# A hybrid attention and expert layer on one core: keys of two head groups packed in one tile, and the rounded products of an attention slot in one run ahead of its attended product

## What is computed

```
x = x + attn_a(layernorm(x))      16 heads, DK = 16, DV = 64
x = x + ffn(layernorm(x))         32 experts (top 8, grouped), one shared expert
x = x + attn_b(layernorm(x))      32 softmax taps of a banded sum
x = x + ffn(layernorm(x))

attn_a:  q, k, v = l2norm of the heads of x@Wq, x@Wkv
         sim  = q . k  per head            (256 x 256)
         attn = square(relu(sim))
         out  = tanh_norm(attn @ v)        tanh(|o|) * o/|o|
         return out (heads side by side) @ Wout
```

## Time and profile before

| | |
|---|---|
| median of 3 runs | 580.83 us (580.67 to 581.53) |
| profiled execution | 580.82 us, of which the span is 579.0 us |
| mean granted TensorE clock | 0.984 |
| busy in the span | PE 536.2 us (93%), PEld 407.0, DVE 424.5, ACT 381.3, POOL 329.6 |
| attention stage | to about 240 us; its batches b=2, 3 start their first factor product at 79.11 and 107.15 us |
| expert stage | from 241.5 us |

### The profile page before, as it was taken

How to read it: one execution, slowest core, us unless ns; L and a number is a source line. 1 busy time by engine, 2 the same in 40 slices (tenths; PEclk the granted TensorE clock), 3 DMA queues, 4 the chain that set the end, 5 groups by cost and what they waited for, 6 DMA issues and landing times. The chain is left out here.

```text
span 579.0 us, 10233 instructions
## 1 busy us (share of the span) xinstructions
PE 536.2 (93%) x3328; PEld 407.0 (70%) x3328; DVE 424.5 (73%) x998; ACT 381.3 (66%) x681; POOL 329.6 (57%) x279
## 2 busy tenths in 40 slices
PE   4678989999999998799999999999999999999996
PEld 4446556666666676487788787787787787888884
DVE  3827697877878688557958869669669668677664
ACT  4749868686868795454565775775775775655653
POOL 1527567483939293167646756656645656566563
PEclk9879999999999999889999999999999999999999
DMA  8200000000000000750076391580660761761930
GB/s 244 69 7 22 9 21 17 16 15 15 15 15 23 13 18 16 183 119 2 5 160 133 102 196 26 138 162 25 166 135 23 168 133 42 170 144 33 214 69 19
DMA packets 35797, 44.89 MB, mean 78 GB/s; under 512 B 5408, under 2 KB 18848, under 8 KB 35744
## 3 DMA queue, kind: packets, MB, share of 16 engines
q1 hardware_dynamic: 31328, 42.66, 32.4%
q10 hardware_dynamic: 4416, 1.57, 1.1%
HBM read 41.07 MB, written 3.15 MB: 76 GB/s over the span
## 5 line engine op out<-in xcount | busy, mean ns | idle before, releaser
L480 POOL TENSOR_TENSOR hl<-hb,hh 128x512 fp32r<-128x512 f32 x128 | 165.4, 1293 | 137.4 <-ACT hh L686 130.7
L679 ACT ACTIVATE sil<-PS 128x512 f32<-128x512 f32 (+1 forms) x136 | 80.8, 594 | 84.8 <-PE PS L1150 84.0
L1029 DVE TENSOR_TENSOR PS<-sil,PS 128x512 f32<-128x512 f32 x128 | 88.3, 690 | 60.3 <-PE PS L1150 38.9
L1150 PE MATMUL PS<-fxh,wfh 128*128 128x512 f32 x264 | 104.8, 397 | 1.7 <-issue 1.7
L1150 PE MATMUL PS<-fxh,wfl 128*128 128x512 f32 x264 | 104.5, 396 | 0.0
L1150 PE MATMUL PS<-fxl,wfh 128*128 128x512 f32 x264 | 104.5, 396 | 0.0
L686 ACT ACTIVATE hh<-hb 128x512 fp32r<-128x512 f32 x128 | 80.3, 628 | 33.1 <-DVE hb L1034 32.7
L1034 DVE TENSOR_TENSOR hb<-PS,wbc 128x512 f32<-128x512 f32 x128 | 88.5, 691 | 11.8 <-issue 3.6
L837 DVE SCALAR_TENSOR_TENSOR aT<-PS,rl 128x1024 f32<-128x1024 f32 x64 | 75.2, 1218 | 8.5 <-ACT rl L543 8.5
L543 ACT ACTIVATE rl<-PS 128x1024 f32<-128x1024 f32 x64 | 62.3, 1031 | 17.7 <-PE PS L1150 17.2
L1150 PE MATMUL PS<-aT,v 128*64 128x256 f32 x512 | 64.0, 393 | 6.0 <-POOL v L409 4.8
(11 more groups left out here) (163 smaller groups left out, 926.0 us busy)
## 6 DMA issues: line engine op xcount, KB each, us to landing
wbc<-w_dram SPq DMA_DIRECT2D x48, 512.0 KB, 11.7
wbc<-w_dram SPq DMA_DIRECT2D x32, 128.0 KB, 2.9
wbc<-w_dram SPq DMA_DIRECT2D x16, 256.0 KB, 4.4
wfs<-wf_dram SPq DMA_DIRECT2D x32, 98.0 KB, 1.9
band_dram<-zero SPq DMA_DIRECT2D x16, 80.0 KB, 1.7
band<-band_dram ACTq DMA_DIRECT2D x4, 320.0 KB, 3.0
out_dram<-X SPq DMA_DIRECT2D x4, 256.0 KB, 2.3
X<-x_dram SPq DMA_DIRECT2D x1, 896.0 KB, 8.1
```

The lines of the kernel that those rows point to most:

```text
L480: g.tensor_tensor(hl[:, n % RING, :], hb[:, n % RING, :], hh[:, n % RING, :].bitcast(F32), ALU.subtract).then_inc(F("hl"), 1)
L679: s.activation(sil[0:rows, n % 2, :], PS[0:rows, G0 + n % 2, :], ACT.Silu).then_inc(F("silu"), 1)
L1029: v_.tensor_tensor(PS[:, bank, :], sil[:, n % 2, :], PS[:, bank, :], ALU.mult).then_inc(F("t"), 1)
L1150: return nc.tensor.matmul(o, w, m, start=start, stop=stop)
```

## The change

Three things are done.

1. *Packed keys.* The 16 rows of zeros in a head's slot of 32 are used: the keys of groups 0 and 1 (and of 2 and 3) stand in the two halves of one key tile, and the queries of a group stand in its half with zeros in the other. So a batch has six tiles of 128 columns (Q0, Q1, K01, K23, Q2, Q3) in NQ = 3 group products for eight tiles in four. Weights have 256 columns less, ACT keeps three copies for four. `score` reads a key tile and a query tile and waits for both.
2. *Order.* The two `values(n, 0, *)` move ahead of `attend(4b)` on PE and ahead of `keep_output(4b)` on ACT; `values(n, 1, 1)` moves ahead of `transpose_norms`; the third group product moves ahead of `attend(4b+2)`, its copy ahead of `keep_output(4b+2)`. The list of turns follows. DVE's order stays as it is.
3. *Factor products.* `spread_factors` does two groups at a time, taking turns between them, and waits for both banks first.

The diff:

```diff
@@ -37,7 +37,10 @@
 BW = P + K
 QK = H * DK
 
-WQ_G, WK_G, W_QK, W_V = 0, NG * P, 2 * NG * P, 2 * NG * P + 2 * QK
+NQ = NG // 2 + 1
+WQ_G, WK_G = (0, 1, 4, 5), (2, 3)
+W_QK = 2 * NQ * P
+W_V = W_QK + 2 * QK
 WA = W_V + H * DV
 
 WG0, WU0, WD0, WS0 = 0, NE * P, 2 * NE * P, 3 * NE * P
@@ -84,15 +87,15 @@
     def late(q, *names):
         return list(names) if q >= 0 else []
 
-    order += [("g", 0, g) for g in range(NG)] + [("qk", 0, 0), ("qk", 0, 1)]
+    order += [("g", 0, j) for j in range(NQ)] + [("qk", 0, 0), ("qk", 0, 1)]
     order += [("v", 0, 0, 0), ("v", 0, 0, 1), ("v", 0, 1, 0), ("v", 0, 1, 1), ("xT", 1)]
     for b in range(B):
         n, q, r = b + 1, b - 1, b - 2
         order += late(r, ("F", r, 2), ("F", r, 3))
         order += coming(n, ("qk", n, 0), ("qk", n, 1), ("v", n, 0, 0), ("v", n, 0, 1)) + late(q, ("nb", q))
-        order += coming(n, ("v", n, 1, 0)) + late(q, ("nt", q)) + coming(n, ("v", n, 1, 1))
+        order += coming(n, ("v", n, 1, 0), ("v", n, 1, 1)) + late(q, ("nt", q))
         order += ([("px", 0)] if b == B - 2 else []) + ([("pc", 0)] if b == B - 1 else []) + late(r, ("y", r, 0))
-        order += coming(n, ("g", n, 0), ("g", n, 1), ("g", n, 2), ("g", n, 3))
+        order += coming(n, ("g", n, 0), ("g", n, 1), ("g", n, 2))
         order += coming(n + 1, ("xT", n + 1)) + late(q, ("ft", q)) + late(r, ("y", r, 1))
         order += ([("pl", 0)] if b == B - 2 else []) + late(q, ("F", q, 0), ("F", q, 1))
     for k, job in enumerate(order):
...
@@ -529,10 +532,10 @@
                 after(act, A("n2q"), 2 * (n - 1) + t + 1)
                 s.activation(sqqk[:, t, :], PS[:, bank_of("qk", n, t), :], ACT.Square).then_inc(free_of("qk", n, t), 1)
 
-            def keep_group(n, g):
-                act.wait_ge(*full("g", n, g))
-                after(act, A("S"), 2 * (NG * (n - 1) + g + 1))
-                s.activation(qk[:, g, :], PS[:, bank_of("g", n, g), :], ACT.Copy).then_inc(free_of("g", n, g), 1)
+            def keep_group(n, j):
+                act.wait_ge(*full("g", n, j))
+                after(act, A("S"), 2 * (NG * (n - 1) + (2 if j == 0 else NG)))
+                s.activation(qk[:, j, :], PS[:, bank_of("g", n, j), :], ACT.Copy).then_inc(free_of("g", n, j), 1)
 
             def relu(i):
                 if i >= NS:
...
@@ -622,10 +624,9 @@
                 if more:
                     square_pairs(n, 0)
                     square_pairs(n, 1)
-                keep_output(NG * b)
-                if more:
                     keep_values(n, 0, 0)
                     keep_values(n, 0, 1)
+                keep_output(NG * b)
                 if b:
                     keep_norms(q)
                 weight_high(NG * b)
@@ -648,10 +649,8 @@
                 if more:
                     keep_group(n, 0)
                     keep_group(n, 1)
+                    keep_group(n, 2)
                 keep_output(NG * b + 2)
-                if more:
-                    keep_group(n, 2)
-                    keep_group(n, 3)
                 if b:
                     tanh_norms(q)
                 weight_high(NG * b + 2)
@@ -1182,10 +1181,10 @@
                 bank, done = turn("qk", n, t)
                 by_token(n, t, W_QK, bank).then_inc(done, 1)
 
-            def group(n, g):
-                bank, done = turn("g", n, g)
-                for part, w0 in enumerate((WQ_G, WK_G)):
-                    cols = slice(w0 + g * P, w0 + (g + 1) * P)
+            def group(n, j):
+                bank, done = turn("g", n, j)
+                for part in range(2):
+                    cols = slice((2 * j + part) * P, (2 * j + part + 1) * P)
                     last = split3(PS[:, bank, part * L:(part + 1) * L], wah[:, cols], wal[:, cols],
                                   xTh[:, :], xTl[:, :])
                 last.then_inc(done, 1)
@@ -1194,13 +1193,15 @@
                 if i >= NS:
                     return
                 b, g = divmod(i, NG)
-                pe.wait_ge(*freed("g", b, g))
+                jq, q0, k0 = WQ_G[g] // 2, WQ_G[g] % 2 * L, g // 2 * L
+                pe.wait_ge(*freed("g", b, jq))
+                pe.wait_ge(*freed("g", b, 1))
                 after(pe, A("a"), 2 * i)
                 for jt in range(2):
                     for s in range(HG):
                         rows = slice(SLOT * s, SLOT * (s + 1))
-                        last = mm(PS[:, S0 + s, jt * L:(jt + 1) * L], qk[rows, g, L + jt * P:L + (jt + 1) * P],
-                                  qk[rows, g, 0:L], True, True)
+                        last = mm(PS[:, S0 + s, jt * L:(jt + 1) * L], qk[rows, 1, k0 + jt * P:k0 + (jt + 1) * P],
+                                  qk[rows, jq, q0:q0 + L], True, True)
                         if jt == 1 and s % 2 == 1:
                             last.then_inc(A("S"), 1)
 
@@ -1241,13 +1242,16 @@
                     last = nc.tensor.transpose(PS[:, bank, it * P:(it + 1) * P], Fpad[:, it, :], ident[:, :])
                 last.then_inc(done, 1)
 
-            def spread_factors(q, g):
+            def spread_factors(q, pair_of_groups):
                 pe.wait_ge(*freed("ft", q))
-                bank, done = turn("F", q, g)
-                rows = slice(SLOT * g, SLOT * (g + 1))
+                groups = (2 * pair_of_groups, 2 * pair_of_groups + 1)
+                turns_of = [turn("F", q, g) for g in groups]
                 for s in range(2):
-                    last = mm(PS[:, bank, s * L:(s + 1) * L], sel[rows, s, :], FT[rows, :], True, True)
-                last.then_inc(done, 1)
+                    for g, (bank, done) in zip(groups, turns_of):
+                        rows = slice(SLOT * g, SLOT * (g + 1))
+                        last = mm(PS[:, bank, s * L:(s + 1) * L], sel[rows, s, :], FT[rows, :], True, True)
+                        if s == 1:
+                            last.then_inc(done, 1)
 
             def project(q, it):
                 for g in range(NG):
...
@@ -1303,26 +1307,23 @@
                 more, last_batch = n < B, b == B - 1
                 score(NG * b + 1)
                 if r >= 0:
-                    spread_factors(r, 2)
-                    spread_factors(r, 3)
+                    spread_factors(r, 1)
                 if more:
                     pe.wait_ge(*freed("xT", n))
                     pairs(n, 0)
                     pairs(n, 1)
-                attend(NG * b)
-                if more:
                     values(n, 0, 0)
                     values(n, 0, 1)
+                attend(NG * b)
                 if b:
                     norms(q)
 
                 score(NG * b + 2)
                 if more:
                     values(n, 1, 0)
+                    values(n, 1, 1)
                 if b:
                     transpose_norms(q)
-                if more:
-                    values(n, 1, 1)
                 attend(NG * b + 1)
                 if b == B - 2:
                     prep_transpose(0)
@@ -1335,10 +1336,8 @@
                 if more:
                     group(n, 0)
                     group(n, 1)
+                    group(n, 2)
                 attend(NG * b + 2)
-                if more:
-                    group(n, 2)
-                    group(n, 3)
 
                 score(NG * b + 4)
                 if n + 1 < B:
@@ -1352,7 +1351,6 @@
                     prep_logits(0)
                 if b:
                     spread_factors(q, 0)
-                    spread_factors(q, 1)
 
             def gate_up(u, p):
                 n = pair(u, p)
@@ -1454,8 +1452,7 @@
                         down(u, 0)
                     if first:
                         if p == 0:
-                            spread_factors(B - 2, 2)
-                            spread_factors(B - 2, 3)
+                            spread_factors(B - 2, 1)
                             norms(B - 1)
                         if p == 1:
                             project(B - 2, 0)
@@ -1467,10 +1464,8 @@
                             transpose_factors(B - 1)
                         if p == 11:
                             spread_factors(B - 1, 0)
+                        if p == 13:
                             spread_factors(B - 1, 1)
-                        if p == 13:
-                            spread_factors(B - 1, 2)
-                            spread_factors(B - 1, 3)
                         if p in (15, 16):
                             project(B - 1, p - 15)
                     if 2 <= u < NC + 2 and p == 0:
@@ -1510,11 +1505,12 @@
     wq = np.asarray(L0_attn_a_Wq)
     wkv = np.asarray(L0_attn_a_Wkv).reshape(D, H, DK + DV)
     wk, wv = wkv[:, :, :DK], wkv[:, :, DK:]
-    q_slots = np.zeros((D, H, SLOT), np.float32)
-    k_slots = np.zeros((D, H, SLOT), np.float32)
-    q_slots[:, :, :DK] = wq.reshape(D, H, DK)
-    k_slots[:, :, :DK] = wk
-    wa = np.concatenate([q_slots.reshape(D, H * SLOT), k_slots.reshape(D, H * SLOT), wq, wk.reshape(D, H * DK), wv.reshape(D, H * DV)], axis=1)
```

(17 more changed lines are left out.)

## The result

| | before | after |
|---|---|---|
| median, in turns on one chip | 580.75 us (578.88 to 581.53, 4 runs) | 592.98 us (590.94 to 593.67, 4 runs) |
| ratio to before | | 1.0222, 95% interval 1.0194 to 1.0250 |
| profiled execution (span) | 580.82 us (579.0) | 593.67 us (591.9) |
| mean granted clock | 0.984 | 0.970 |

The account below looks back on a forecast made before the run. TensorE was taken to bound a batch, DVE and ACT close behind. Head -2.0, stall +6.8 and clock +8.5 gave +13.3 us on 580.8: 594.1 us, range 581 to 601 (own range 588 to 600, chance 0.48).

Parts of the forecast that it names:

- The wait before g2: TensorE, batches b=2 to 6: the third group product (g2) waits 3.3 us for DVE's X to free its bank.
- Its price: Batches b=2 to 6: the wait before g2 makes each batch 1.35 us longer, +6.8 us in all (2.0 to 7.2).
- The clock: TensorE at half clock behind each new wait in five batches: 1.7 us each, +8.5 us (0 to 17).
- Rival B: Batches b=2 to 6: the stall alone, the clock mostly holds; +4.8 us, 585.6 us; chance 0.24.
- The head: Start and b=0: fewer group matmuls, a smaller load, two value products moved into the 4.76 us wait; -2.0 us.
- The factor pairs: Factor products on TensorE: interleaving in pairs costs nothing, since the next product waits for a bank that DVE frees.
- The packed keys and y0: TensorE, each batch: six matmuls go, 0.72 us; the 0.58 us wait ahead of the first projection (y0) goes.
- Behind b=7: b=7 has no coming products: 0 us; the expert stage behind it is not edited.

Follow-up runs that it names:

- the filled kernel: Changed kernel with the second group product made five times in batches 2 to 6, to fill TensorE's wait ahead of the third; 584.88 us, ratio 1.0083 to before.
- norms between: Changed kernel with the transposed norms back between the two value products of slot 4b+2 on TensorE; 587.52 us, ratio 1.0131 to before.
- X earlier: Changed kernel with DVE's add_attention(r, 0), which frees the third group product's bank, moved ahead of squares(4b+3); 572.26 us, ratio 0.9855 to before.
- both: Changed kernel with DVE's add_attention(r, 0) directly behind clear_norms(n, 0) and the transposed norms back between the value products; 564.17 us, ratio 0.9724 to before.
- g2 behind: Changed kernel with the third group product and its ACT copy back behind attend(4b+2) and keep_output(4b+2); 573.20 us, ratio 0.9873 to before.
- X first, norms late: Changed kernel with add_attention(r, 0) directly behind clear_norms(n, 0) and DVE's n2o copy behind the squares of slot 4b+2; 570.96 us, ratio 0.9841 to before.
- the last two kernels: The kernels of the last two experiments on the changed kernel: "both", 564.17 us, and "X first, norms late", 570.96 us.

## Why the prediction was right, step by step

**The wait before g2: right, 3.10 us for 3.3.** Its mechanism, the bank held for X, is shown twice: the wait falls to 0.83 us and then to nothing as X is written earlier, and TensorE is busy instead when work is put there. That DVE's chain sets its length is shown by the norms moved back (0.70 us less). The size came out by parts that were a little off and partly cancelled: the transposed norms start 2.57 us behind score(4b+2), not 2.77, so that squares of that slot start 11.12 us into the batch and not at 11.36 (before: 11.17); X ends so that g2 starts at 20.36 and not 20.66. TensorE was ready for it at 126.34, 17.26 into the batch, for 17.4.

**Its price: 1.1 us a batch for 1.35,** so 5.5 us for 6.8, if b=3 stands for all five. Two ways gave it, both in b=3: the filled kernel, and the one with the norms between. Most of the difference is that g2 starts 0.3 us earlier than the sum had it.

**The clock: 9.9 us for 8.5.** It is what is left of the 15.4 us in the five batches. Each of the five waits (3.08, 3.10, 3.53, 3.10, 2.52 us) had a stretch of 3.4 us behind it, at about 1.9 us (b=3) where 1.7 was taken; that is the mis-sized term. Two things make up the 1.9. From g2 to score(4b+4) are 4.31 us for 2.78 in the filled kernel: 1.5 us for the products at half rate. From that score to the next batch are 5.87 us for 5.47, though the clock is 1.00 again. The prediction had nothing new late there (5.48 us), but the half clock makes the attended product late, and with it tanh on ACT, so that DVE's `ff` falls beside POOL's scaling of values (134.26 to 136.16), takes 1.03 us and pushes `xTl` to the end of the batch. DVE in b=3:

```profile
135.18 1.03 DVE L855 TENSOR_TENSOR ff<-f,th 128x32 f32<-128x32 f32 x1 [3.50 <-ACT th L572]
...
139.11 0.41 DVE L810 TENSOR_TENSOR xTl<-PS,xTh 128x256 fp32r<-128x256 f32 x1
```

The next batch's factor product, whose bank `xTl` frees, starts at 139.62, 0.10 us behind its end. That this is where the 0.4 us come from is read from the rows; no run took it alone.

The stretch at 78.18 us stands behind waits of 1.28 and 1.68 us at the end of b=1, where before had 0.42, 1.09 and 0.31, and makes b=2 31.61 us long instead of 30.54. The prediction looked for the clock's risk at g2 alone. The filled kernel has the same two waits (1.26 and 1.67 us) and no stretch behind them, and the packed keys alone have shorter ones (1.15 and 1.09 us) and a stretch, so this one looks like chance. 5 x 1.9 + 1.1 would be 10.6, 0.7 us more than 9.9: 0.5 of it is that b=2 was 0.5 us longer than b=3 already before, and the rest is in b=4 (0.35 us under 1.1 + 1.9) and b=6 (0.25 over). The Trainium skill (TensorE: Matmul & The Clock Gate, "HAM oscillation") says that a loop with waits between its bursts can fall back in each round; the trace of the changed kernel agrees, five rounds of five; with the norms between it was two of five. Rival B, the stall without the clock, is near what the filled kernel makes: 28.65 us in b=3 for B's 28.9. That its 584.88 us also meet B's 585.6 is partly luck, since b=4 and b=6 are long for another reason. B fell because all five waits were followed by half clock.

**The head: -1.64 us for -2.0.** The first attended product starts at 31.38 us (30.8 to 32.6 predicted), with 3.16 us of wait for 4.76.

**The factor pairs: nothing, right.** The next product starts 1.94 us behind the first factor product, 1.97 before. The Trainium skill's rule on packing small matmuls (same page, "Part 3: Packing small matmuls") brought nothing here, where the next product waits for a bank.

**The packed keys and y0: right.** 0.71 us a batch for 0.72, and the wait of 0.58 us is gone. ACT's relu came 1.1 us earlier in the batch (8.94 for 10.09) and helped nobody, as predicted.

**Behind b=7: -0.9 us where I had 0.** The wait of 1.70 us ahead of the first expert product is the same in both, but the half clock behind it lasts 3.4 us and not 6.8: from that product to the end of the span are 336.4 us for 337.5. This is chance, not the change (below), and it happens to cancel the 1.1 us of the stretch at 78.18 us.

That the sum came within 1.1 us of the median is in part luck: the stall came 1.3 us under, the clock 1.4 us over, the head 0.4 us over and the end 0.9 us under, which cancels to 0.4 us in the profiled execution.

## What to carry to other kernels

A product that is moved ahead of other work also takes its buffer's release with it: list what frees the bank, on which engine, and what stands ahead of that release in its queue, and move the release too (here one DVE instruction, worth 20 us). Where a loop has such a wait, price it twice, once as idle time and once for the half clock behind it, and try more work in the gap before the order is given up. An order that measures slower can be the better one with one release missing; the packed keys alone gave 4 us, and together with the order, its release and the norms moved they gave 16.

## What the runs showed of the hardware that I had not expected

**The same wait of about 2 us is sometimes followed by half clock and sometimes not.** Of the waits ahead of g2, those of 2.52 us and more were followed by 0.50 each time (six of six, one of them in the kernel with the norms between), those of 2.18 to 2.40 us in one of four, those of 1.64 and less in none. The wait of 1.67 or 1.68 us ahead of batch b=2 was followed by it in four kernels (after, X earlier, norms between, both) and not in two (g2 behind, stall filled); in the kernel of the packed keys alone a stretch from about 78.5 to 82 us follows waits of only 1.15 and 1.09 us, where before had 0.42 and 1.09 us and no stretch. Ahead of the first expert product every kernel has the same 1.69 to 1.70 us of wait, and the rest of the span shows what follows ("both" is X first with the norms between):

| half clock behind it | kernels | from that product to the end of the span |
|---|---|---|
| none | g2 behind; packed keys alone; both | 335.1, 335.1, 334.8 us |
| 3.4 us | after; stall filled | 336.4, 336.5 us |
| 6.8 us | before; X earlier; norms between | 337.5, 337.5, 337.5 us |
| 10.2 us | X first, norms late | 339.7 us |

So what follows this one wait moves a profiled execution by up to 5 us, with no change in the code there but the order of a few factor products. The two kernels that came out 3 and 2 us under what I expected have no half clock there in their profiles, and the one 2 us over has the longest; but the packed keys alone have none either and came out as expected, so this bears on the misses without settling them. What decides it the runs don't show.

**A small DVE operation can be held by POOL.** In batch b=3 `nmx` (128x32) takes 0.17 us in the last two kernels, and 1.77 at 129.30 in the changed one, where POOL's scaling of values runs from 129.13 to 131.03. `Fpad` and `ff` above are held in the same way. In the attention stages of the nine profiles, 62 operations of DVE on 128x32 (tensor_scalar, tensor_tensor and cast) started more than 0.02 us into such a scaling and more than 0.1 us ahead of its end, and all 62 ended 0.03 to 0.06 us behind its end, after 0.50 to 1.90 us. Nine reciprocals beside it kept their 0.35 us, and X, which reads one operand from PSUM, its 0.28. So an operation that moves by a few tenths can cost over 1 us more: in the filled kernel this made two of five batches long. No run changed POOL's work, so the coupling is read from such coincidences alone.
